# Mixture-of-experts block on one NeuronCore: roots per expert tile, routing ahead of the shared expert, and row additions that wait for the preceding tile only where token ids meet

## What is computed

```python
hs = einsum('bct,bcd->bdt', x, cond_w[cond])           # 128 x 32 x 256
t = hs.reshape(4096, 256)
scores = sigmoid(t @ gate_w.T)                          # 32 experts in 4 groups of 8
sb = scores + gate_bias
group = top2(sb of the group).sum()                     # 2 groups of 4 are kept
topi = top_k(sb where the group is kept, 8)             # 8 experts of the 16
wsel = scores[topi]; wsel = wsel / wsel.sum() * 2.5
cw = zeros(4096, 32).at[topi].add(wsel)
h = relu(einsum('tl,eil->eti', t @ fc1_w.T, w1)) ** 2 * cw.T[:, :, None]
routed = einsum('eti,eli->tl', h, w2) @ fc2_w.T         # latent width 128
shared = relu(t @ shared_up_w.T) ** 2 @ shared_down_w.T # inner width 512
out = x + shared + routed
```

## Time and profile before

| | |
|---|---|
| median of 3 runs | 437.25 us (436.96 to 437.43) |
| the profiled execution, own time | 437.96 us |
| span from first to last instruction | 436.2 us |
| busy: TensorE, VectorE, ScalarE, POOL | 383.4, 307.4, 253.5, 200.5 us |
| mean granted TensorE clock | 0.963 of 2.4 GHz |

### The profile page before, as it was taken

The page is one execution under the profiler, slowest core; times in us unless marked ns, Lnnn a source line. Parts: engine busy times, 40 slices in busy tenths (PEclk is TensorE's granted clock), DMA queues, the critical chain, the costliest instruction groups (busy, mean ns, idle before and its releaser), DMA issues. The chain is left out here.

```text
span 436.2 us, 6956 instructions
## 1 busy us (share of the span) xinstructions
PE 383.4 (88%) x2224; PEld 332.0 (76%) x2224; DVE 307.4 (70%) x581; ACT 253.5 (58%) x330; POOL 200.5 (46%) x153
## 2 busy tenths in 40 slices
PE   8798989998799667999999999999999999998520
PEld 8787988998689565788888888888888888888410
DVE  0258999999998514788778778778787787875300
ACT  1364445555365503677777877778777778775300
POOL 5000076857777400014544467563564345533561
PEclk9999999999999969899999999999999999999955
DMA  6992573942943788768988998999998899989542
GB/s 172 252 294 68 191 256 104 303 137 83 347 140 117 243 235 251 228 199 197 227 223 218 217 216 219 225 239 340 345 324 231 219 223 321 349 214 259 81 41 31
DMA packets 66249, 93.55 MB, mean 214 GB/s; under 512 B 19295, under 2 KB 48086, under 8 KB 65622
## 3 DMA queue, kind: packets, MB, share of 16 engines
q1 hardware_dynamic: 52210, 77.71, 55.6%
q0 software_dynamic: 13296, 15.08, 20.6%
q10 hardware_dynamic: 708, 0.32, 0.3%
HBM read 94.48 MB, written 30.18 MB: 286 GB/s over the span
## 5 line engine op out<-in xcount | busy, mean ns | idle before, releaser
L530 POOL DMA_INDIRECT out_x<-res,sid_sb x70 | 123.2, 1759 | 159.6 <-DMA out_x<-res,sid_sb 71.6
L1011 DVE TENSOR_TENSOR act_lo<-act_full,act_hi 128x1024 fp32r<-128x1024 f32 (+3 forms) x92 | 106.0, 1152 | 25.3 <-ACT act_full L874 21.0
L1274 DVE SCALAR_TENSOR_TENSOR scaled<-h_banks,cond_bd 128x1024 f32<-128x1024 f32 (+3 forms) x76 | 86.5, 1138 | 40.2 <-PE h_banks L694 39.9
L694 PE MATMUL h_banks<-xc_hi,w_ring 128*128 128x512 f32 (+3 forms) x304 | 95.2, 396 | 3.0 <-issue 0.8
L509 POOL DMA_INDIRECT rows_dram<-payload,slot_idx x64 | 70.2, 1097 | 47.9 <-DVE payload L1149 25.3
L715 PE MATMUL y_banks<-act_hi,w_ring 128*128 128x512 f32 (+3 forms) x304 | 78.0, 379 | 5.6 <-ACT act_hi L872 5.6
L872 ACT ACTIVATE act_hi<-scaled 128x1024 fp32r<-128x1024 f32 (+3 forms) x76 | 75.0, 986 | 2.6 <-PE y_banks L715 1.7
L874 ACT ACTIVATE act_full<-scaled 128x1024 f32<-128x1024 f32 (+3 forms) x76 | 74.7, 983 | 0.0
L715 PEld LDWEIGHTS y_banks<-act_hi,w_ring 128*128 128x128 f32 x304 | 55.5, 190 | 16.7 <-ACT act_hi L872 5.2
L694 PEld LDWEIGHTS h_banks<-xc_hi,w_ring 128*128 128x128 f32 x304 | 51.6, 191 | 15.0 <-issue 6.0
L694 PE MATMUL h_banks<-xc_lo,w_ring 128*128 128x512 f32 (+3 forms) x152 | 57.8, 380 | 0.0
(11 more groups left out here) (147 smaller groups left out, 617.4 us busy)
## 6 DMA issues: line engine op xcount, KB each, us to landing
w_ring<-w_dram SPq DMA_DIRECT2D x76, 512.0 KB
cond_bd<-s_dram SPq DMA_DIRECT2D x64, 512.0 KB, 5.5
w_dram<-w_ring SPq DMA_DIRECT2D x8, 1024.0 KB, 7.0
x_in<-in_x SPq DMA_DIRECT2D x8, 512.0 KB, 6.6
res<-in_experts_raw SPq DMA_DIRECT2D x4, 1024.0 KB, 10.6
out_x<-x_in SPq DMA_DIRECT2D x8, 512.0 KB, 3.7
rows_sb<-rows_dram SPq DMA_DIRECT2D x16, 256.0 KB, 5.3
rows_dram<-in_pad_rows SPq DMA_DIRECT2D x5, 328.0 KB, 4.4
```

What stands on the lines that cost most here:

```text
L530: pool.indirect_dma_start(out, bass.IndirectOffsetOnAxis(ap=sid_sb[:, i % SID_RING, j, GROUP_SIZE:PER_GROUP], axis=0), res[:, i % 2, j * H ...
L694: last = pe.matmul(h_banks[:, s, m * BANK:m * BANK + SIZE[i]], w, v, start=n == 0, stop=n == 2)
L1011: dve.tensor_tensor(lo, full, hi.bitcast(f32), ALU.subtract).then_inc(act_lo_ready, 1)
L1274: dve.scalar_tensor_tensor(pair(scaled, i, u), h, 0.0, scale, ALU.max, ALU.mult).then_inc(scaled_ready, 1)
```

## The change

Three things change.

1. **Roots per tile.** roots(k) goes from VectorE. combine_weights writes the weights themselves to the payload, with one small multiply more. After transpose_s(i) ScalarE makes a seed by its function Abs_reciprocal_sqrt and a copy, and POOL does one Newton round on 36 partitions x 128 (root_s, four instructions). store_s waits for it; it is on ScalarE's queue for tiles 0 to 2 and on SP's from tile 3 on. root_s(0) to (3) stand ahead of the first addition on POOL, root_s(i + 4) between the second and the third addition of tile i.
2. **Routing ahead.** BATCH_BLOCKS becomes [1, 2, 2, 2, 1], SCORES_RING 5, the wait inside scatter goes, and the orders of TensorE, ScalarE, VectorE and SP are written anew: projections, gates and routing come earlier, shared_down and its sums later. At the crossing the order is shared_up(14), transpose_s(0), shared_down(12), transpose_x(0), shared_down(13), shared_up(15), shared_down(14), experts_up(0, 0), shared_down(15), transpose_s(1).
3. **Additions.** out_added becomes two semaphores, for even and odd tiles. A tile waits for the additions of tile i - 2. From tile 3 on POOL reads the first and last id of each tile into registers and waits for the tile before only if the two ranges of ids meet. Tiles 1 and 2 always wait.

The diff, cut:

```diff
-BATCH_BLOCKS = [2, 2, 2, 1, 1]
+ROOTS_AHEAD = 4
+BATCH_BLOCKS = [1, 2, 2, 2, 1]
-SCORES_RING = 4
+SCORES_RING = 5
...
+        def store_s(queue, i):
+            queue.wait_ge(s_rooted, i + 1)
+            dst = s_dram[i % S_RING, 0:PER_GROUP * SIZE[i]].rearrange("(e j t) -> j e t", e=PER_GROUP, t=P)
+            queue.dma_start(dst, s_part[0:ROWS_OF[i] * PER_GROUP, i % 2, :]).then_inc(s_stored[i % S_RING], DMA)
...
             for u in range(PAIRS):
                 load_weights(0, u)
+            store_shared(3)
             store_split(3)
+            store_shared(4)
             sp.wait_ge(pads_stored, GROUPS * DMA)
             sp.wait_ge(dummy_stored, DMA)
             sp.wait_ge(rows_scattered, scatters(BATCHES - 1))
...
             load_rows(1)
-            store_shared(6)
+            for i in range(2, 4):
+                read_table(i)
+                load_sid(i)
+            store_shared(5)
             for u in range(PAIRS):
                 load_scale(0, u)
+            load_rows(2)
+            store_shared(6)
             read_group(1)
             splits_stored(1)
             for u in range(PAIRS):
                 load_weights(1, u)
...
                         if i > 0:
                             load_weights(i + 1, u)
+                    if u == 2 and i + 2 < X_TILES and i > 0:
+                        store_s(sp, i + 2)
...
                 for n in range(FIRST_TILE[k], FIRST_TILE[k + 1]):
-                    if n == FIRST_TILE[k] + BT and k < 2:
-                        pool.wait_ge(rows_scattered, TOP_GROUPS * n * DMA)
...
+            def root_s(i):
+                pool.wait_ge(s_seeded, i + 1)
+                pool.wait_ge(s_t_copied, i + 1)
+                part, seed, guess, rest_of = (t[0:ROWS_OF[i] * PER_GROUP, i % 2, :] for t in (s_part, s_seed, s_guess, s_rest))
+                pool.tensor_tensor(guess, part, seed, ALU.mult).then_inc(root_step, 1)
+                pool.wait_ge(root_step, 3 * i + 1)
+                pool.tensor_tensor(rest_of, guess, seed, ALU.mult).then_inc(root_step, 1)
+                pool.wait_ge(root_step, 3 * i + 2)
+                pool.tensor_scalar(rest_of, rest_of, -0.5, 1.5, ALU.mult, ALU.add).then_inc(root_step, 1)
+                pool.wait_ge(root_step, 3 * i + 3)
+                pool.tensor_tensor(part, guess, rest_of, ALU.mult).then_inc(s_rooted, 1)
+            for i in range(ROOTS_AHEAD):
+                root_s(i)
...
+            def read_ids(i):
+                ids_of = sid_sb[:, i % SID_RING, :, GROUP_SIZE:PER_GROUP]
+                lowest.append(pool.value_load(ids_of[0:1, 0, :], min_val=0, max_val=TOKENS + BANK - 1))
+                highest.append(pool.value_load(ids_of[P - 1:P, ROWS_OF[i] - 1, :], min_val=0, max_val=TOKENS + BANK - 1))
+            def wait_for_shared_tokens(i):
+                reaches = (highest[i - 1] - lowest[i] + (1 << ID_BITS)) >> ID_BITS
+                starts = (highest[i] - lowest[i - 1] + (1 << ID_BITS)) >> ID_BITS
+                meets = (reaches & starts) & 1
+                pool.wait_ge(out_added[(i - 1) % 2], (ADDS_BY[i - 3] + meets * ROWS_OF[i - 1]) * DMA)
+                pool.sem_inc(tokens_apart, 1)
             for i in range(X_TILES):
                 pool.wait_ge(sid_loaded[i % SID_RING], (i // SID_RING + 1) * DMA)
-                if i > 0:
-                    pool.wait_ge(out_added, ADDS_TO[i] * DMA)
+                read_ids(i)
+                if i >= 2:
+                    pool.wait_ge(out_added[i % 2], ADDS_BY[i - 2] * DMA)
+                if i >= 3:
+                    wait_for_shared_tokens(i)
+                elif i > 0:
+                    pool.wait_ge(out_added[(i - 1) % 2], ADDS_BY[i - 1] * DMA)
                 for j in range(ROWS_OF[i]):
+                    if j == 2 and i + ROOTS_AHEAD < X_TILES:
+                        root_s(i + ROOTS_AHEAD)
...
@@ ScalarE @@
+                act.activation(s_seed[of, i % 2, :], t_banks[of, 0, 0:P], ACT.Abs_reciprocal_sqrt, bias=TINY).then_inc(s_seeded, 1)
+                act.activation(s_part[of, i % 2, :], t_banks[of, 0, 0:P], ACT.Copy).then_inc(s_t_copied, 1)
...
             latent_and_scores(7)
+            act.activation(table_load[:, :], zero[:, :], ACT.Abs_reciprocal_sqrt, bias=TINY).then_inc(table_loaded, 1)
...
+            copy_s(0)
+            square_shared(14)
+            store_s(act, 0)
+            round_x(0)
+            relu_shared(15)
...
@@ VectorE @@
-                dve.scalar_tensor_tensor(cw[:, 0:NT[k], :], work[:, 0:NT[k], :], ROUTED_SCALE,
...
-                for _ in range(ROOT_STEPS):
...
+                step(dve.tensor_scalar(total[:, 0:NT[k]], total[:, 0:NT[k]], ROUTED_SCALE, None, ALU.mult))
...
             group_scores(0)
+            rest_of_projection(2)
             pick_groups(0)
-            rest(0)
+            rest_of_projection(3)
             largest(0)
             mark(0)
+            combine_weights(0)
+            group_scores(1)
             read_rank(0)
             slot_of_token(0)
-            roots(0)
...
             slot_of_token(1)
+            rest(0)
+            rest(1)
+            rest_of_weights(0)
```

More of the change, by code:

```diff
@@ L53 @@
 PARTS_TO = [sum(PARTS[:n]) for n in range(X_TILES + 1)]
[L54 removed]
+ADDS_BY = [sum(ROWS_OF[n % 2:n + 1:2]) for n in range(X_TILES)]
+ID_BITS = 13
 REGION = TOKENS + BANK
```

273 lines of the change are left out of this document (119 added, 154 removed).

## The result

The changed kernel takes 421.11 us (median of 4 runs, 419.82 to 423.11), against 437.11 for the kernel before on the same chip: a ratio of 0.9639, with a 95% interval of [0.9596, 0.9681]. The forecast was 413.3 in a range of 404 to 428. So it is 16 to 19 us faster by the medians and 16 to 22 by the ratios, where 24 were forecast. As a ratio the forecast is 413.3 / 437.25 = 0.945, outside the first interval and inside the second. The two intervals are of one and the same kernel and don't meet; their middles lie 1.5%, or 6.6 us, apart.

A forecast was written before the change was run, and what follows sets the result against it. TensorE was taken to bound the steady expert tiles, leaving gains in first-stretch gaps, crossing and tail. Start 17 plus additions 7, roots 0, made 24 us off 437.96: 414 profiled, 413.3 at the median, range 404 to 428.

The forecast's parts named there:

- the forecast case: Main case for the whole kernel's time, 406 to 420 us, given a chance of 0.65.
- the backlog stays: Rival: root, id reads and additions fill POOL, tail gains 2, weight loads stall 3; 423 us, chance 0.2.
- The start: First stretch, crossing and pipeline fill: stall 7.7, slow clock 1.9, fill 4.4, gaps 3.0; 17.0 us, ends 12 and 20.
- the layout: New queue order laid out with the old durations; leaves 6 of the first stretch's 10.6 us of TensorE gaps.
- The stall of 7.73 us: At the crossing, TensorE's wait for the ids of tile 0 goes entirely, ids being 10 us early: 7.7 us.
- the 13.4: Expert tiles: x transposes stay 13.33 us apart; a spacing above 13.4 makes the prediction wrong.
- The roots: Expert tiles: POOL's root steps, 1.6 to 2 us with waits, are covered by slack; counted 0, bound -3.
- the prediction's price: Expert tiles: VectorE's rest blocking POOL's root steps costs some 0.2 us each, under a microsecond per tile.
- The additions: Tail: tiles 14 and 15 add when their res is there, so chain 16 to 18 starts earlier; 7.0 us, bounds 2 and 11.
- POOL becomes the clock: Rival, expert tiles: root steps and reads above 5.1 us per tile push POOL past 13.33; 486 us at upper ends, chance 0.06.
- The table load at every seed: Rival, expert tiles: two table loads a tile, 2.6 us or more, eat ScalarE's 3.3; 420 to 450 us, chance 0.04.
- the start that gives nothing: Rival, first stretch: routing is ahead but starved, only stall and tail gain; 427.6 us, chance 0.05.

The follow-up runs named there:

- The second: The changed kernel, unchanged, measured again on another chip against the kernel before: 418.34 us, ratio 0.9489.
- the first profile: Profile of the changed kernel's 423.11 us run, span 421.3, from its first measurement against the kernel before: 421.11 us.
- the bias early: Changed kernel with SyncE's load of the gate's bias moved ahead of the x loads of blocks 2 and 3 and the first raw weights: 416.33 us.
- the run that puts it before the wait: Changed kernel with the additions part undone and the root put ahead of the wait for the preceding tile's landing: 421.79 us, ratio 0.9653.
- the additions part alone: Kernel before with only the third part of the change added; roots stay on VectorE and the first half's order stays: 431.68 us against 438.26.
- the chained: Changed kernel with its third part undone, so every tile's additions wait for all of the preceding tile's: 432.22 us, ratio 0.9847.
- the GpSimd-stored: Changed kernel with every store of the shares issued by GpSimd right behind its root: 431.46 us, ratio 0.986.
- the doubly moved: Changed kernel with its third part undone and SyncE's store of the shares moved four steps later: 457.60 us, ratio 1.046.

## Why the prediction was right, and where it fell short

**The number.** 421.11 lies in the range of 404 to 428, but that range is wide, and the first measurement is outside the forecast case (406 to 420) and next to the 423 of "the backlog stays". The second, 418.34, is inside the case. Two of the three terms came out near their size, and the third, put at nothing, did not.

**The start, 17.0 forecast.** Measured up to tile 4: 13.0 in the first profile, 16.7 in the second, 18.8 with the bias early. TensorE's gaps ahead of the ids' transpose, 10.6 us before and 6 in the layout, are 8.7, 6.7 and 5.0 us in these three. The size was about right, the layout of the queues had a hole: it left out that group_scores(0) now needs the bias before block 2's low parts, and that SyncE issues it behind two x loads and the raw weights. In the profile before VectorE waits for no bias, as its routing comes later.

**The steps on the way.** The last scatter was forecast at 121 to 124 and is at 135.4 (131.1 to 133.2 in the later profiles). Only part of that is the late first scatter. The other part is a mis-sized term: the sum took 0.98 + 0.30 us for each of 64 scatters, the shortest rows, while they are 1.42 apart on average, (135.42 - 45.68) / 63. It cost nothing, since the ids' transpose waits for nothing even so. The stall of 7.73 us and the slow clock behind it went as said: the clock is 1.00 in the crossing. The x transposes of tiles 3 to 11 keep their spacing, (296.17 - 189.17) / 8 = 13.38, but one later step takes 14.41 us (309.52 to 323.93), and from tile 4 to 15 the mean is 13.46, just over the 13.4 that the prediction named as a sign of being wrong.

**The roots, 0 forecast with a bound of -3.** This is the step that failed. Seed and table came out as forecast, one more table load of 1.28 us, and so did the steps where nothing disturbs them, 0.29 to 0.46 us. But a root takes 3.1 us of GpSimd in its place, 3.3 with the waits between its steps, not 1.6 to 2. Its first step averages 1.26 us over the expert tiles behind an addition, and 0.59 in the run that puts it before the wait. And its cost isn't its length. The prediction gave SyncE's store the slack of the loads behind it as cover and counted 0, but the root behind the store stands behind the landing of an addition, and holds SyncE's weight loads with it. At tile 16 TensorE waits 2.08 or 3.13 us for weights and then runs in part at the lower clock, and tile 15's result comes 3.7 to 4.8 us later than without: more than the bound of -3. So the gain behind tile 15 is 3.3 or 2.5 us, where the additions part alone brings 6.7.

**Where a root meets VectorE.** The step of 1.33 us above begins at 212.82; VectorE's rest of two SBUF inputs ran 212.37 to 213.83 (1.46 us, not its usual 1.22), and the step ended 0.32 us later:

```profile
212.37 1.46 DVE L1054 TENSOR_TENSOR act_lo<-act_full,act_hi 128x1024 fp32r<-128x1024 f32 x1
```

Two other long steps (198.62 for 1.94, 226.23 for 1.37) ended 0.30 and 0.31 us behind such a rest as well, though these two rests took their usual 1.22. By the page "SBUF — State Buffer" of the Trainium skill (Who interferes with whom) the two block each other, and the trace agrees. Each of the 15 roots behind an addition has one such step, lengthened by 0.2 to 0.9 us. An estimate from these rows: of the 3.06 us of a mean root 1.65 are the four steps undisturbed, 0.6 the first step's place behind an issue (1.03 at the least, 0.45 undisturbed), and 0.8 the rest. So the prediction's price, under a microsecond per tile, holds.

**The additions, 7.0 forecast.** Right by itself (6.6 alone), and the meets and the ones apart were as computed: tiles 3, 6, 8, 9 and 15 wait for ScalarE only, and 11 and 14 run on without a wait. At tile 7 the profile names a landing (3.01 us), but the addition goes 0.27 us behind the end of its own result's copy, as at 3, 6, 8 and 9. Tile 15 had no backlog: its result was copied at 382.92, and its first addition went at 383.98. The sum had the landing of its last addition at 3.0 to 7.4 us, and it took 8.8 beside the loads of tile 18's weights. That alone doesn't explain the shortfall, as the additions part alone has the same 9.6 us from that addition to tile 16's first and still gains its 6.7.

**The rivals.** "The backlog stays", with a chance of 0.2 and 423 us, named the root of tile 17 holding SyncE's loads for tile 16 and 3 us on TensorE, and that happened (2.08 and 3.13 us at tile 16). Its backlog in the additions was gone by tile 15. "POOL becomes the clock" was off by its price (3.3 us, below the 5.1 at which it starts), but the chained, the GpSimd-stored and the doubly moved kernels show how near it lay. The table load at every seed and the start that gives nothing did not come.

## What to carry to other kernels

A piece of work put on another engine is paid where it stands in that engine's order, not by its length: placed behind a wait, it hands that wait to everyone who needs it, here from an addition's landing through a root and a store to the weight loads. Put such work ahead of the wait, in its shadow (8 to 10 us in the chained kernel). And when a stage is moved earlier, list every input it needs by its place in the issuing queue, the smallest too: a bias behind three large loads held the first routing.

## What the runs showed of the hardware

- A GpSimd operation right behind the issue of an indirect DMA has a longer row: the first step of a root 1.03 us at the least, while the addition's own row of 1.55 us still runs, and 0.45 to 0.63 elsewhere.
- An addition to DRAM lands in 3.7 to 3.8 us on quiet queues (the chain 16, 17, 18) and in 6.3 to 8.8 between 384 and 392 us beside the last weight loads, with 208 GB/s moved in the first profile and 270 in the second.
- A wait of 2 to 3 us in the middle of the expert tiles costs TensorE more than its length: behind 3.13 us it was granted 0.62 of its clock for 4.5 us.
- A small DMA behind large ones on its queue lands at a varying time: the same wait for the bias was 2.5 to 6.6 us in eight profiles of kernels with the same first half, and the x of tile 1 came at 158.5 to 163.35, though not in step with it (2.9 us and 161.15 in one).
